# Map pieces of an expert layer respaced, and a routing step split into bf16 codes first and weights later

## The reference, cut to what matters

```python
logits = jnp.clip(xt @ gate_w.T, -50.0, 50.0)
top_w, top_idx = jax.lax.top_k(logits, TOP_K)          # TOP_K = 2
rw = jax.nn.softmax(top_w, axis=-1)
deltas = jax.nn.softmax(expert_atom_weights, axis=-1) @ atoms
weighted = deltas * jax.nn.sigmoid(importance)         # 8 experts x 4096 places
vals = jnp.einsum('tk,tks->ts', rw, weighted[top_idx])
contrib = jax.ops.segment_sum((xg * vals).T, rows, num_segments=H)
out = xt @ W.T + contrib.T
```

```python
routed = jnp.einsum('te,tei,eih->th', routing_weight, jax.nn.silu(g) * u, wd)   # 16 experts, 4 per token
shared = jax.nn.silu(x @ sg) * (x @ su) @ sd
```

## Time and profile before

| what | value |
|---|---|
| time before, median of 3 runs (lowest, highest) | 2150.16 us (2141.95, 2152.39) |
| the profiled execution: its own time, its span | 2149.47 us, 2147.5 us |
| TensorE / VectorE / ScalarE / GpSimd busy | 87% / 55% / 43% / 45% of the span |
| layer b | about 650 to 1488 us |
| layer d | about 1925 us to the end |

### The profile page before, as it was taken

How to read it: one execution, slowest core, us unless ns; L and a number is a source line. 1 busy time by engine, 2 the same in 40 slices (tenths; PEclk the granted TensorE clock), 3 DMA queues, 4 the chain that set the end, 5 groups by cost and what they waited for, 6 DMA issues and landing times. The chain is left out here.

```text
span 2147.5 us, 38657 instructions
## 1 busy us (share of the span) xinstructions
PE 1864.9 (87%) x11487; PEld 1422.2 (66%) x11487; DVE 1177.1 (55%) x2617; ACT 927.9 (43%) x2627; POOL 961.3 (45%) x1011
## 2 busy tenths in 40 slices
PE   4688999999987877799999999995879999886992
PEld 1355666665546777799999999894456665545782
DVE  5566776776654655332222244332867777864445
ACT  3367676776642321222222233331266666641110
POOL 1478777887711324214334333332265445411561
PEclk9899999999988988899999999998889999996996
DMA  8578877778716417658897898654344454529657
GB/s 318 180 234 279 264 238 222 250 244 263 245 30 227 93 45 145 204 177 234 254 288 204 241 288 235 173 128 96 110 108 101 109 116 110 124 55 389 228 165 271
DMA packets 231726, 412.51 MB, mean 192 GB/s; under 512 B 45082, under 2 KB 119195, under 8 KB 226212
## 3 DMA queue, kind: packets, MB, share of 16 engines
q1 hardware_dynamic: 165164, 322.28, 47.6%
q0 software_dynamic: 30592, 62.08, 12.9%
q10 hardware_dynamic: 35776, 25.69, 4.9%
HBM read 211.97 MB, written 155.52 MB: 171 GB/s over the span
## 5 line engine op out<-in xcount | busy, mean ns | idle before, releaser
L702 ACT ACTIVATE a_P<-a_SC,a_nm 128x256 f32<-128x256 f32 x512 | 235.9, 473 | 132.1 <-DVE a_nm L604 130.5
L1220 POOL DMA_INDIRECT b_y_rows<-b_ysb,b_entry x79 | 124.5, 1575 | 342.9 <-ACT b_ysb L1368 196.5
L604 DVE TENSOR_REDUCE a_nm<-a_SC 128x2 f32<-128x512 f32 x256 | 164.8, 685 | 142.3 <-PE a_SC L835 141.0
L567 POOL TENSOR_TENSOR a_praw<-a_praw,a_phigh 128x704 f32<-128x704 f32 (+2 forms) x126 | 192.0, 1524 | 10.3
L1472 DVE TENSOR_TENSOR b_xl<-b_XT,b_xh 128x512 fp32r<-128x512 f32 x97 | 67.0, 691 | 219.8 <-ACT b_xh L1374 215.5
L846 PEld LDWEIGHTS a_T<-ident,a_P 128*128 128x128 f32 x1024 | 119.4, 145 | 79.7 <-issue 48.2
L846 PE MATMUL a_T<-ident,a_P 128*128 128x128 f32 x1024 | 147.9, 283 | 21.8 <-DVE a_PT L616 18.2
L1478 DVE TENSOR_TENSOR b_al<-b_AT,b_ah 128x384 fp32r<-128x384 f32 x111 | 61.9, 557 | 188.5 <-ACT b_ah L1379 170.9
L1379 ACT ACTIVATE b_ah<-b_AT 128x384 fp32r<-128x384 f32 x111 | 54.6, 492 | 241.0 <-PE b_AT L1304 187.4
L565 POOL CAST a_phigh<-a_praw 128x704 fp32r<-128x704 f32 (+2 forms) x126 | 112.2, 890 | 96.7 <-DMA a_praw<-in_L_ffn_wg 29.7
L2197 ACT ACTIVATE c_P<-c_SC,c_nm 128x240 f32<-128x240 f32 x256 | 115.7, 457 | 76.8 <-DVE c_P L2069 76.8
(11 more groups left out here) (490 smaller groups left out, 4935.1 us busy)
## 6 DMA issues: line engine op xcount, KB each, us to landing
w_parts<-a_phigh SPq DMA_DIRECT2D x72, 352.0 KB
w_parts<-a_praw SPq DMA_DIRECT2D x72, 352.0 KB, 3.9
b_wh<-w_parts SPq DMA_DIRECT2D x18, 1216.0 KB
b_wl<-w_parts SPq DMA_DIRECT2D x18, 1216.0 KB
c_q<-c_qT SPq DMA_DIRECT2D x64, 256.0 KB
c_k<-c_kT SPq DMA_DIRECT2D x124, 128.0 KB
b_wh<-w_parts SPq DMA_DIRECT2D x18, 704.0 KB
b_wl<-w_parts SPq DMA_DIRECT2D x18, 704.0 KB
```

What stands on the lines that cost most here:

```text
L567: eng.tensor_tensor(raw[:, 0:k * m], raw[:, 0:k * m], r32(high[:, 0:k * m]), ALU.subtract).then_inc(plow_done, 1)
L604: eng.tensor_reduce(nm[:, g % 4, j, :], SC[j][:, :].rearrange("p (t k) -> p t k", t=BT), AX.X, ALU.max, negate=True).then_inc(topped, 1)
L702: e = eng.activation(Pr[:, i, t, :], SC[j][:, t * S:(t + 1) * S], ACT.Exp, bias=nm[:, g % 4, j, t:t + 1], accum_out=den[:, h, t:t + 1])
L1220: eng.indirect_dma_start(out=y_rows, out_offset=bass.IndirectOffsetOnAxis(ap=entry[:, r, 1:2].bitcast(U32), axis=0), in_=ysb[:, v % RING, ...
```

## The change

In layer b one line: four pieces eight steps apart in the dense steps (2, 10, 18, 26), then twelve pieces six steps apart from step 34 (34, 40, ..., 100).

```diff
-    MDENSE, MSTEP = 7, 4
-    MAP_AT = {2 + MSTEP * i if i < MDENSE else NU - MSTEP * (MAPS - i): i for i in range(MAPS)}
+    MDENSE, DENSE_STEP, MSTEP = 4, 8, 6
+    MAP_AT = {2 + DENSE_STEP * i if i < MDENSE else DENSE + 2 + MSTEP * (i - MDENSE): i for i in range(MAPS)}
```

```diff
 def entries():
+    eng.wait_ge(codes_made, CODES)
     for j in range(PICKS):
-        if j % NT == 0:
-            eng.wait_ge(picks_made, j // NT + 1)
         if j % CHUNK == 0:
             eng.wait_ge(placed, j // CHUNK + 1)
-        m = eng.matmul(EN[:, :], place[:, j, :], picked[:, j, :, :].rearrange("p c r -> p (c r)"),
+        m = eng.matmul(EN[:, :], place[:, j, :], codes[:, j, :, :].rearrange("p c r -> p (c r)"),
...
+def entry_weights():
+    eng.wait_ge(picks_made, 1)
+    for j in range(PICKS):
+        m = eng.matmul(EW, place[:, j, :], picked[:, j, :, :].rearrange("p c r -> p (c r)"),
...
+def one_hots():
+    eng.tensor_tensor(in_unit[:, :, :], unit_of[:, :].unsqueeze(1).to_broadcast([P, PICKS, NR]),
+                      at_unit[:, :].unsqueeze(2).to_broadcast([P, PICKS, NR]), ALU.is_equal).then_inc(vseq, c.inc())
+    eng.wait_ge(vseq, c.now)
+    eng.tensor_tensor(codes[:, :, 0, :], in_unit[:, :, :], group[:, :, :], ALU.mult).then_inc(codes_made, 1)
+    eng.tensor_scalar(codes[:, :, 1, :], in_unit[:, :, :], lane[:, 0:1], None, ALU.mult).then_inc(codes_made, 1)
+    for j in range(PICKS):
+        e = eng.tensor_scalar(place[:, j, :], place_of[:, :], at_place[:, j:j + 1], None, ALU.is_equal)
...
+def share_picks():
+    eng.tensor_tensor(picked[:, :, :, :], in_unit[:, :, :].unsqueeze(2).to_broadcast([P, PICKS, PARTS, NR]),
...
-for i in range(len(PARTS)):
-    count_chosen(i)
+for g in range(NG):
+    count_chosen(g)
 entries()
+entry_weights()
...
-for k in range(K):
-    picks(k)
-make_plan()
-rows()
-eng.wait_ge(vseq, c.now)
+one_hots()
+share_split()
+rows()
+share_picks()
+make_plan()
 rows_low_(0)
+weights()
```

More of the change, by code:

```diff
@@ L2624, in routed_maps @@
     HOME = NT - BT
-    PARTS = ((0, NT - GT), (NT - GT, NT))
     COLS = 32
@@ L2653, in routed_maps @@
         xT_at = nc.sbuf_base - 4 * WIDE * D
-        place = shared("place", [P, PICKS, BLOCK], F32, xT_at)
+        codes = shared("codes", [P, PICKS, CODES, NR], BF16, xT_at)
+        place = shared("place", [P, PICKS, BLOCK], BF16, xT_at + 4 * 4 * D)
         unit_parts = shared("unit_parts", [P, 2, 2, KD, P], F32R, xT_at)
@@ L2681, in routed_maps @@
         ysb = sb("ysb", [P, RING, D])
-        picked = shared("picked", [P, PICKS, 2, NR], F32, nc.sbuf_base - 4 * RING * D)
-        assert 2 * NR * PICKS <= RING * D
+        ysb_at = nc.sbuf_base - 4 * RING * D
+        picked = shared("picked", [P, PICKS, PARTS, NR], BF16, ysb_at)
+        group_i = shared("group_i", [P, PICKS, NR], I32, ysb_at)
+        group = shared("group", [P, PICKS, NR], BF16, ysb_at + 2 * PARTS * PICKS * NR)
+        assert 2 * (PARTS + 1) * PICKS * NR <= 4 * RING * D and CODES * PICKS * NR <= 8 * D
         XT = [ctx.enter_context(nc.psum_tensor(f"d_XT{i}", [P, KD * P], F32)) for i in range(2)]
-        LG = [ctx.enter_context(nc.psum_tensor(f"d_LG{i}", [P, (b - a) * COLS], F32))
-              for i, (a, b) in enumerate(PARTS)]
+        LG = [ctx.enter_context(nc.psum_tensor(f"d_LG{i}", [P, GT * COLS], F32)) for i in range(2)]
         R = ctx.enter_context(nc.psum_tensor("d_R", [P, (NT + 1) * E], F32))
-        EN = ctx.enter_context(nc.psum_tensor("d_EN", [P, 2 * NR], F32))
+        EN = ctx.enter_context(nc.psum_tensor("d_EN", [P, CODES * NR], F32))
         Y = [ctx.enter_context(nc.psum_tensor(f"d_Y{i}", [P, D], F32)) for i in range(2)]
@@ L2692, in routed_maps @@
         LGT = [y[:, 0:P] for y in Y]
-        gw_cleared, lg_copied, lg_turned = sem("gw_cleared"), sem("lg_copied"), sem("lg_turned")
+        EW = LG[0][:, 0:PARTS * NR]
+        gw_cleared, lg_copied, lg_turned, lg_read = [
+            sem(n) for n in ("gw_cleared", "lg_copied", "lg_turned", "lg_read")]
         gw_in, maps_in, maps_ready = sem("gw_in"), [sem(f"maps_in{e}") for e in range(E)], sem("maps_ready")
@@ L3027, in picks @@
-                for j in range(k * NT, (k + 1) * NT, CHUNK):
-                    eng.tensor_tensor(place[:, j:j + CHUNK, :],
-                                      place_of[:, :].unsqueeze(1).to_broadcast([P, CHUNK, BLOCK]),
-                                      at_place[:, j:j + CHUNK].unsqueeze(2).to_broadcast([P, CHUNK, BLOCK]),
-                                      ALU.is_equal).then_inc(placed, 1)
+                eng.tensor_tensor(codes[:, :, 0, :], in_unit[:, :, :], group[:, :, :], ALU.mult).then_inc(codes_made, 1)
@@ L3087, in _ @@
             eng.tensor_copy(pad[:, :], pad_i[:, :]).then_inc(vseq, c.inc())
-            eng.tensor_copy(code_w[:, :, 0], code_i[:, :]).then_inc(vseq, c.inc())
+            eng.tensor_copy(lane[:, :], lane_i[:, :]).then_inc(vseq, c.inc())
+            eng.tensor_copy(place_of[:, :], place_i[:, :]).then_inc(vseq, c.inc())
             eng.wait_ge(vseq, c.now)
-            for i in range(len(PARTS)):
-                chosen_of(i)
+            for g in range(NG):
+                chosen_of(g)
             eng.wait_ge(vseq, c.now)
```

93 lines of the change are left out of this document (59 added, 34 removed).

## The result

The changed kernel takes 2125.56 us (median of 4 runs, 2122.59 to 2131.64); the kernel before, beside it, 2146.48 us (median of 4). The ratio is 0.9904, with a 95% interval of 0.9883 to 0.9926: about 21 us faster, and the predicted time of 2132 is 0.3% off.

What follows compares the result with a forecast made beforehand. TensorE's step was taken to bound layer b, with 57 us lost around small-write groups, and SyncE's map-load issues layer d's start. 2149.47 - 4 - 8 - 6 + 0.9 + 0 = 2132.4, said as 2132; range 2107 to 2147.

Steps and rivals of the forecast that it cites:

- Layer d, 0: Layer d: rows land about 5 us earlier, but SyncE's last map-load issue bounds the first unit; 0, bounds -1 and +3.
- The choice by groups: VectorE in layer d: four parts of 2.87 us end at 1948.0 against 1946.9, one-hots at 1951.5 instead of 1950.15.
- the rows land 6.3 us after the first issue: Layer d: gather starts at 1963 to 1965 instead of 1969.15, rows land at 1969 to 1971 instead of 1975.48.
- The cover of 3 us: TensorE in layer d: after the weights' matmuls and turning rows it is ready at 1976, before the first unit at 1978.89.
- Routed steps, -6 + 0.9: Layer b's routed steps: a table-load wait goes, 6 us gained; three more pieces at 0.3 each cost 0.9.
- the 2.7: Layer b's routed steps: what is left of 8.7 us lost after the table-load wait, taken as 0.3 a piece.
- The rival in which these steps pay: Layer b's routed steps: blocked load issues cost 7 us each; with six such pieces 2174; chance 0.07.
- Third group, -8: Layer b, steps 16 to 20: the wait for a late table load goes, 8 us gained; bounds 1 and 15.1.
- First group, -4: Layer b, steps 9 to 12: the pieces' stores and load leave this group, 4 us gained, between 0 and 14.3.
- Second and fourth, 0: Layer b, steps 12 to 16 and 20 to 23: the pieces stay as they are there, so 0.
- the rival in which the pieces' DMAs stall the groups: Layer b's dense steps: the first and third group then lose nothing, -14.3 and -15.1, giving 2115; chance 0.20.
- Small writes alone: Layer b's dense steps: small writes alone stall the groups, first keeps 14.3, third ends at 14.0; -6.2, 2143; chance 0.27.

Runs made afterwards that it cites:

- Layer d alone: The kernel before with the whole diff of layer d and the old spacing of map pieces, against the kernel before: 2123.77 us, ratio 1.0001.
- sets 1 and 3: Two of three sets of four experiments, each on another chip with the kernel before run beside it: that kernel's median was 2124.38 and 2133.15 us.
- set 1: The first four experiments, on one chip, all edits of the kernel before, which had a median of 2124.38 us beside them.
- the first measurement: The changed kernel against the kernel before, ahead of the three sets of experiments: 2125.56 against 2146.48 us, ratio 0.9904.
- set 2: Four experiments on another chip: the changed kernel again, with writes paced, with maps known early, and the kernel before with two load buffers; kernel before 2143.71 us.
- layer b's line alone: The kernel before with only the new spacing of map pieces, layer d as before, against the kernel before: 2089.97 us, ratio 0.9839.
- plan-first kernel: The changed kernel with two VectorE calls swapped, make_plan ahead of share_picks, small writes not paced: 2087.45 us, one run.
- paced and early kernel: The changed kernel with small writes spread four to a step and maps_ready raised three experts behind SyncE's issues, against the kernel before: 2101.07 us, ratio 0.9848.

## Why the prediction was right, and where it was not

**Layer d, 0: right, and shown.** Layer d alone gives 1.0001, and the distance to unit 0 stays at 53.6 to 54.0. That `maps_ready` and not routing ends the wait is shown by raising it earlier: unit 0 comes 2.65 us sooner and the layer is 3.7 us shorter. The working held in most parts. The tables were to be done 34.8 to 36.7 us after the layer's first instruction: 1943.68 - 1907.43 = 36.3. The gather was to start after 37.7 to 39.7: 38.9. The weights' matmuls were to end after 47.3: 45.4, at 0.10 each instead of 0.13. The choice by groups was undersized: the one-hots begin 28.3 us after the layer's start, not 26.2. One step of the working failed, that the rows land 6.3 us after the first issue and so 5 us earlier. TensorE turns them after 48.3 us against 50.2 before, 1.9 earlier, since the first issue took 4.08 us beside the product. The cover of 3 us was right in size (3.37 us of waiting for the signal, of which 2.65 came free in the experiment), but by luck: I had worked it out behind the weights' matmuls, and these ended at 1952.81, 2.9 us before the rows were there.

**Routed steps, -6 + 0.9: right, too small.** From 8.7 to 1.3 us lost, -7.4. The long wait for a late load went, and most of the 2.7 that I put down to the pieces themselves went with it. The rival in which these steps pay did not come about: five issues of loads took 3.9 to 6.2 us each, and the 75 steps lost 1.3 in all. No issue there came near the 12.99 from which the rival was priced, so what one that long would cost was not seen.

**Third group, -8: right in kind.** The late load's wait is gone, the group loses 9.4 instead of 15.1 (-5.7). One reason that I gave is wrong: a copy does stand at steps 18 and 19 with the new spacing too (2, 10, 18, 26). What changed is that its load is issued at step 13 and not at step 17. First group, -4: -2.9. Second and fourth, 0: -0.5 and -4.0. Together -13.0 where -12 stood, in this pair of profiles. That the sum fits is luck: the fourth group's -4.0, for which I had put 0, makes up for what the first and third fell short.

**The step that failed** is under these numbers: what a group costs, and why. I took a group's loss as one thing, 12 to 15.7 us wherever it fell, of which the pieces might hold a share. There are at least two, and the runs part them.

- *Late loads.* On the chips of sets 1 and 3, the old spacing waits 21.0 to 45.5 us for table loads in the dense steps, and no copy there waits with pieces eight apart. In set 1 this is nearly the whole loss (26.3 us with 35.2 of waits, to -0.6). It lies in the first, third and fourth group (6.9, 11.1 and 9.0), of which I had put 0 for the fourth. With some 8 us of the routed steps, layer b's line is worth 34 us there, 1.6%. That is the size of the rival in which the pieces' DMAs stall the groups (2115, 34 us off), but by another split: it took 29.4 from the first and third group alone. Part of the third group's loss is not the wait for a load but the load's issue, which held ScalarE in four of the five profiles with the old spacing (12.99, 7.62, 9.76 and 9.84 us).
- *Remote waits.* The two profiles of the first measurement and all four of set 2 have them (19 to 54 us); the eight of sets 1 and 3 have 0 to 5.9. The changed kernel's own layer b is on both sides of this: 37 and 54 us of remote waits in two profiles, none in layer b's line alone and in the plan-first kernel. The change does not remove them, and where they are, a loss of 44 and 30 us stays in the changed kernel's steps 9 to 24 that set 1 does not have. That goes with a first result of 0.990 instead of the 0.984 of set 1. So the forecast time was met on a chip where these waits stayed; on the chip of set 1 the same forecast would have been too small by half.

*Small writes alone* is refuted where it could be tried: without pieces in the dense steps the four bursts cost -0.1 and 3.8 us in two sets, and the -0.6 of layer b's line alone has the bursts as well. Neither of those sets had long remote waits, so where they are long the rival is open. The Trainium skill ("DMA: Bandwidth & Descriptors", section "Specifications") says that transfers under 512 B are done by reading, modifying and writing. That may be so for the 8-byte writes; no run here measures the transfers themselves, and on these chips four bursts cost the engines at most 3.8 us. *The pieces' DMAs stall the groups* is nearer the truth in sets 1 and 3, by another way than I had: not in that an engine's progress is disturbed, but in that ScalarE's program waits for a load that came one step or two after its issue.

**What stays open** is what the remote waits are. Shown: they fall in the stretch of the bursts; ScalarE's input has been ready for 10 us when it goes on; they go with the chip, or with the occasion, and not with the source; pacing the writes took 15 us off the changed kernel on a chip that has them. Not shown: what the engine waits for, whether the pieces' stores lengthen them, and whether the place of the DRAM tables matters. One observation narrows it: TensorE too pauses for "issue" in these steps, 5.3 to 23.8 us in the six profiles with long remote waits and 0 to 2.0 in the other eight, in five of the six also between matmuls of one product. So it is not a late input alone. That the instructions themselves come late is a rival that no run tests. The early steps of the program also scatter by up to 8 us, and step 52 by up to 6, in kernels that are the same up to there. One profile a kernel does not part differences under some 5 us.

## What to carry to other kernels

A copy that waits for a load issued a fixed number of steps before it can have a cliff: here 4 to 4.67 steps between pieces lost up to 45 us in all, while 8 in the dense steps and 6 in the routed ones kept the waits for loads under 3 us each. So give such a chain slack before anything else is tuned, and read it off as the wait of the first consumer. Before an early stage is shortened, find who gives the last signal at its end: here a whole rewritten routing stage was worth nothing, since SyncE signalled only after its last issue. Then measure the stage by its own length as well: the 3.7 us that the earlier signal gave layer d did not show in the kernel's median. And when stalls have no releaser in the profile, run the same kernel on another chip before building on them: with the same layer b, half the loss that I set out to explain was not there.

## What the runs showed of the hardware

- An indirect DMA's issue on GpSimd took 4.08 to 4.22 us (eight profiles) beside a bf16 product with two inputs on VectorE that took 4.05, and 0.95 to 1.07 otherwise; it ended 0.9 us after the product in both orders (after: 1950.37 against 1949.42; plan first: 1907.05 against 1906.20). The Trainium skill ("SBUF — State Buffer", section "SBUF: two separate sides") says that VectorE and GpSimd share a pair of ports, that an instruction of VectorE in some modes or with two inputs in SBUF holds the pair to its end, and that GpSimd, locked out, cannot write its DMA's descriptors. The times of the trace agree; it does not show the ports. Many small instructions of VectorE (32 of 0.17 us) were not seen to do this, as no gather stood beside them.
- The issue of a 512 KB load from ScalarE's queue took 0.40 us for the first piece, 0.60 us for most, and up to 12.99 before and 9.84 in the experiments; after the `b_silu` that ran at the start of the 12.99 (until 815.74), ScalarE did nothing until the issue was over (827.08).
- A load of 512 KB took 29.6 us from issue to use (802.40 to 831.99) in the dense steps with the old spacing and writes paced. In the paced and early kernel one took 29.9 us to land, 8.79 of them its issue, and no copy waited for it, as its copy came five steps later.
- One kernel's median differed by 0.9% between chips (2124.38 and 2143.71 us).
